# Macaron block on one core: the start-up DMAs move to SyncE, the weight setup becomes a planned step, and the whole order is replanned

## The reference

```
x = x + 0.5 * ffn(layernorm(x), gate_w, gate_b, w1, b1, w2, b2)      # stage A
x = x + attn(layernorm(x), Wq, Wkv_down, Wk_up, Wv_up, Wo)           # stage B
x = x + 0.5 * ffn(layernorm(x), gate_w, gate_b, w1, b1, w2, b2)      # stage C, the same weights

ffn:  probs = softmax(x @ gate_w.T + gate_b);  the 2 best of 8 experts
      y = sum over the 2 of prob * (relu(x @ w1[e] + b1[e]) @ w2[e] + b2[e])   # hidden size 256
attn: q = x @ Wq.T;  k, v = (x @ Wkv_down.T) @ W_up.T;  8 heads of 32, softmax over 512 tokens
```

## Time and profile before

| | |
|---|---|
| median of 3 runs | 1355.59 us (1354.84 to 1357.04) |
| the profiled execution | 1360.36 us, span 1358.6 us |
| mean granted TensorE clock | 0.948 of full |
| busy: PE | 1216.4 us (90%) |
| busy: DVE, POOL, ACT | 822.4, 795.4, 712.1 us |
| DMA | 203.12 MB, mean 150 GB/s |

### The profile page before, as it was taken

The page is one execution under the profiler, slowest core; times in us unless marked ns, Lnnn a source line. Parts: engine busy times, 40 slices in busy tenths (PEclk is TensorE's granted clock), DMA queues, the critical chain, the costliest instruction groups (busy, mean ns, idle before and its releaser), DMA issues.

```text
span 1358.6 us, 26424 instructions
## 1 busy us (share of the span) xinstructions
PE 1216.4 (90%) x8853; PEld 804.5 (59%) x8853; DVE 822.4 (61%) x2234; ACT 712.1 (52%) x1469; POOL 795.4 (59%) x783
## 2 busy tenths in 40 slices
PE   2888889999979989989989899999999988989893
PEld 1575466666655555556756565656565655657573
DVE  2745747686577655676638766764677836455242
ACT  1334556656645555656565456666555555545430
POOL 1012674765556757765385667768757675657633
PEclk9877999898989899989999899999998999989997
DMA  9204564762645165425645353544464327657741
GB/s 310 109 8 125 175 192 125 238 188 67 182 147 163 34 194 178 119 82 151 202 144 156 90 171 96 181 132 143 138 180 132 111 64 226 204 172 226 222 152 50
DMA packets 167913, 203.12 MB, mean 150 GB/s; under 512 B 17050, under 2 KB 112482, under 8 KB 167780
## 3 DMA queue, kind: packets, MB, share of 16 engines
q1 hardware_dynamic: 146944, 166.36, 39.9%
q0 software_dynamic: 15360, 31.49, 7.9%
q10 hardware_dynamic: 5476, 3.59, 0.8%
HBM read 153.53 MB, written 47.84 MB: 148 GB/s over the span
## 4 chain that ended last, share of the span: by engine, by line
PE 48%; POOL 15%; DVE 12%; issue 9%; DMA 9%; ACT 4%; ACTq 1%; SPq 1%; POOLq 0%; DVEq 0%
PE psum L1455 42%; POOL pairs L955 7%; POOL Y L1006 5%; DMA Y<-results_C,posC 4%; POOL slots_C L986 3%; DVE neg_m L1410 3%; DVE X L1394 3%; PE psum L1676 3%; DMA slots_C<-xnC,posC 2%; DMA Y<-results_A,posA 2%; ACT probs L1093 2%; PE psum L1554 1%; PE psum L1619 1%; PE psum L1518 1%; DVE ntC L1262 1%
## 5 line engine op out<-in xcount | busy, mean ns | idle before, releaser
L1410 DVE TENSOR_REDUCE neg_m<-psum 128x1 f32<-128x512 f32 x512 | 317.0, 682 | 175.2 <-PE psum L1455 137.6
L955 POOL TENSOR_TENSOR pairs<-probs 128x512 f32<-128x512 f32 x256 | 321.0, 1277 | 64.6 <-ACT probs L1093 61.1
L1455 PE MATMUL psum<-nat 32*128 32x512 f32 x2048 | 349.3, 641 | 7.0 <-DVE neg_m L1410 3.0
L1093 ACT ACTIVATE probs<-psum 128x512 f32<-128x512 f32 x512 | 264.6, 607 | 94.5 <-PE psum L1455 78.1
L986 POOL DMA_INDIRECT slots_A<-xnA,posA x120 | 117.2, 976 | 194.2 <-DVE posA L1378 84.7
L1455 PEld LDWEIGHTS psum<-nat 32*128 32x128 f32 x2048 | 137.4, 186 | 113.8 <-issue 38.3
L1455 PEld LDWEIGHTS psum<-xg_T,wt 128*128 128x128 f32 x1296 | 161.0, 198 | 40.3 <-issue 20.0
L1006 POOL DMA_INDIRECT Y<-results_C,posC x120 | 116.3, 969 | 114.0 <-DMA Y<-results_C,posC 74.3
L1455 PE MATMUL psum<-xg_T,wt 128*128 128x128 f32 x1296 | 177.9, 287 | 2.6 <-DMA wt<-packed 1.1
L986 POOL DMA_INDIRECT slots_C<-xnC,posC x120 | 118.5, 987 | 92.0 <-DMA slots_C<-xnC,posC 55.5
L1006 POOL DMA_INDIRECT Y<-results_A,posA x120 | 116.0, 967 | 87.2 <-DMA Y<-results_A,posA 51.0
(11 more groups left out here) (191 smaller groups left out, 1602.5 us busy)
## 6 DMA issues: line engine op xcount, KB each, us to landing
wt<-packed SPq DMA_DIRECT2D x324, 320.0 KB
xs<-slots_A SPq DMA_DIRECT2D x36, 256.0 KB
results_A<-ys SPq DMA_DIRECT2D x36, 256.0 KB
xs<-slots_C SPq DMA_DIRECT2D x36, 256.0 KB
results_C<-ys SPq DMA_DIRECT2D x36, 256.0 KB
X<-in_L_attn_x_dram SPq DMA_DIRECT2D x16, 256.0 KB, 5.3
out_dram<-X SPq DMA_DIRECT2D x16, 256.0 KB
packed<-probs SPq DMA_DIRECT2D x1, 2560.0 KB, 7.8
```

The costliest lines, as they stand in the source:

```text
L955: pool.tensor_tensor(pairs[:, kt // 2, j, :], probs[:, kt - 1, j, :], probs[:, kt, j, :], ALU.add).then_inc(S["p_added"], 1)
L1093: act.activation(probs[:, kt, j, :], at.banks()[j][:], ACT.Exp, scale=SCALE).then_inc(a_done, 1)
L1410: V_.tensor_reduce(neg_m[:, g, n, j:j + 1], at.banks()[j][:], AX.X, ALU.max, negate=True).then_inc(d_done, 1)
L1455: return nc.tensor.matmul(dst, w, m, start=start, stop=stop)
```

## The change

- The five attention weights, w1, b1, b2 and w2 are issued by SP in a new step `weights`, planned right behind the load of batch 0. ACT keeps the two gate DMAs, each now with a semaphore of its own.
- b1 comes as one row of 8 KB into one partition (`b1_row`). PE subtracts it from the sums: behind each product of `ones` with w1 follows one of `minus_one` (one row of -1) with `b1_row`, into the same bank. DVE needs one operation for each two experts instead of two.
- The setup is a planned step `setup` with parts on PE, ACT and DVE, behind `weights` and the first `logits`. ACT takes over the copies and high parts (`up_T`, `wqkv_h`, `wo_T`, b2's high parts); DVE keeps the subtractions.
- The gate is centred in two places: transposed before the first `xTf`, summed before the first `logits` (`center_gate`); DVE's `split_gate` runs behind the first `scaled`. POOL makes the identity and `ones` first and signals `ident_made`.
- The zeros are 992 elements wide and each is written 4 times per partition, instead of 256 wide, of which 128 are written 31 times. The second zeroing is planned behind the pack.
- All constants of the wanted times are new; `dh` no longer waits for the first `top1`.

```diff
-PERIOD, FIRST_B = 37.1, 69.39
+PERIOD, FIRST_B = 38.24, 39.26
-GROUP_GAP, MAX_PACE, S_FIRST, S_PACE, PV, ADD, SUM = 16.85, -0.47, 6.42, 3.29, -1.04, 48.06, 7.28
-A_LEAD, A_PACE, A_ROUTE, A_NORMS = 25.07, 8.22, 70.15, 8.3
-C_NORM, C_ROUTE, C_FIRST, C_PACE, C_GATHER = 54.52, 11.03, 52.26, 12.66, 13.88
-LOAD_AHEAD, W_AHEAD = 131.75, -1.62
-B_SHIFT = [-16.68, 10.52, -34.69, 26.01, 19.68, 22.99, -114.09, 39.85, 0.43, 9.81, 13.71, -5.78, -8.53, -28.27, 13.04, 118.28]
-A_SHIFT = [-30.75, -15.91, -16.67, -4.56, -2.89, -0.98, -3.68]
-C_SHIFT = [-12.0, 2.29, 20.79, -2.05, -93.81, 6.84, -64.33]
+GROUP_GAP, MAX_PACE, S_FIRST, S_PACE, PV, ADD, SUM = 15.72, -2.01, 5.9, 3.29, -0.74, 52.24, 4.01
+A_LEAD, A_PACE, A_ROUTE, A_NORMS = 36.46, 7.1, 71.69, 0.82
+C_NORM, C_ROUTE, C_FIRST, C_PACE, C_GATHER = 60.24, 5.64, 53.49, 12.44, 6.3
+LOAD_AHEAD, W_AHEAD = 121.7, -9.5
+B_SHIFT = [-12.96, 25.85, -23.82, 26.67, 22.19, -5.23, -81.66, 37.19, -12.29, -17.82, -36.02, -16.36, -4.18, -18.95, 34.18, 92.52]
+A_SHIFT = [-64.76, -32.85, 8.56, 1.55, 1.67, 0.78, -1.64]
+C_SHIFT = [-6.42, 7.83, 22.01, -28.41, -39.96, -80.33, -60.43]
...
+    "weights": ((("SP", 6.5),), 6.0), "setup": ((("PE", 4.0), ("ACT", 2.5), ("DVE", 6.0)), 0.0),
...
+    wanted["A", 0, "load", 0], wanted["A", 0, "weights", 0], wanted["A", 0, "setup", 0] = -1000.0, -999.0, -998.0
...
-    after(("A", 0, "pack", 0), ("A", 0, "top1", 0))
+    after(("A", 0, "weights", 0), ("A", 0, "load", 0), part=0)
+    after(("A", 0, "setup", 0), ("A", 0, "weights", 0), ("A", 0, "logits", 0))
+    for key in (("A", 0, "pack", 0), ("A", 0, "dh", 0), ("B", 0, "q", 0), ("A", 0, "top1", 0)):
+        after(key, ("A", 0, "setup", 0))
+    first_part(("A", 0, "blank", 0), ("A", 0, "weights", 0))
+    first_part(("A", 0, "blank", 1), ("A", 0, "pack", 0))
...
+            def weights(at):
+
+                for dst, src in (
+                    (wq_raw, wq.rearrange("(g p) d -> p g d", p=P)), (wo_raw, wo),
+                    (wk_raw, wk_up.rearrange("(g p) r -> p g r", p=P)),
+                    (wv_raw, wv_up.rearrange("(g p) r -> p g r", p=P)),
+                    (down_raw, wkv_down),
+                ):
+                    sp.dma_start(dst, src).then_inc(weights_in, 16)
+                sp.dma_start(pack[:, :, 0:HID], w1.rearrange("e p h -> p e h")).then_inc(experts_in, 16)
+                sp.dma_start(b1_row[:, 0:EXPERTS * HID], b1.rearrange("e h -> (e h)").unsqueeze(0)).then_inc(experts_in, 16)
+                for row in (0, B2_LOW):
+                    sp.dma_start(b2_raw[row:row + 1, 0:EXPERTS * D], b2.rearrange("e d -> (e d)").unsqueeze(0)).then_inc(experts_in, 16)
...
-                sp.dma_start(slots[s].rearrange("(p i) d -> p i d", p=P),
-                             zeros[:, 0:D].unsqueeze(1).to_broadcast([P, NT_MAX, D])).then_inc(zero_in[s], 16)
+                sp.dma_start(slots[s].rearrange("(p i) d -> p (i d)", p=P).rearrange("p (f c) -> p f c", f=4),
+                             zeros.unsqueeze(1).to_broadcast([P, 4, NT_MAX * D // 4])).then_inc(zero_in[s], 16)
...
+            def setup(at):
+
+                high_row, low_row = slice(0, 1), slice(B2_LOW, B2_LOW + 1)
+                act.wait_ge(setup_pe, 3)
+                act.activation(up_T, psum[5][0:RANK, :], ACT.Copy).then_inc(setup_act, 1)
...
-                    chain(V_.tensor_tensor(fix, fix, psum[i][:].rearrange("p (e h) -> p e h", e=2), ALU.subtract))
-                    V_.scalar_tensor_tensor(out=own, in0=fix, scalar=1.0 / D, in1=own, op0=ALU.mult, op1=ALU.add).then_inc(setup_dve, 1)
+                    V_.scalar_tensor_tensor(out=own, in0=psum[i][:].rearrange("p (e h) -> p e h", e=2), scalar=-1.0 / D, in1=own,
+                                            op0=ALU.mult, op1=ALU.add).then_inc(setup_dve, 1)
...
-                    pe_mm(psum[i][:].rearrange("p (e h) -> p e h", e=2), ones[:], pack[:, 2 * i:2 * i + 2, 0:HID]).then_inc(setup_pe, 1)
+                    pe_mm(psum[i][:].rearrange("p (e h) -> p e h", e=2), ones[:], pack[:, 2 * i:2 * i + 2, 0:HID], stop=False)
+                    pe_mm(psum[i][:], minus_one[:], b1_row[:, 2 * i * HID:2 * (i + 1) * HID], start=False).then_inc(setup_pe, 1)
...
+            def setup(at):
+
+                before = order["PE"][:order["PE"].index(at.step)]
+                pe.wait_ge(a_done, max(counts["a_full", step] for step in before if step[2] in A_STEPS))
+                pe.wait_ge(d_done, max(counts["d_full", step] for step in before if step[2] in D_STEPS))
+                turn_attention()
+                sum_experts()
```

More of the change, by code:

```diff
@@ L511, in assert_reuse @@
 def assert_reuse(order):
+    at_setup = {engine: order[engine].index(("A", 0, "setup", 0)) for engine in ("PE", "ACT", "DVE")}
+    for ring, engine in RELEASES.items():
+        names = D_STEPS if ring == "d" else A_STEPS
+        assert all(step in order[engine][:at_setup[engine]] for step in order["PE"][:at_setup["PE"]] if step[2] in names)
     at = {engine: {step: n for n, step in enumerate(order[engine])} for engine in ENGINES}
@@ L656, in macaron_kernel @@
     routed = [st[:2] for st in order["DVE"] if st[2] == "top1"]
-    first_steps = order["PE"][:order["PE"].index(("A", 0, "logits", 0)) + 1]
+    scaled_steps = [st for st in order["DVE"] if st[2] == "scaled"]
+    first_steps = order["PE"][:order["PE"].index(("A", 0, "setup", 0))]
     assert all(bank != GATE_BANK for step in first_steps for bank, _ in order["banks"][step])
@@ L1177, in _ @@
             chain = Chain(dve, link)
[L1179 to L1184 removed]
+            V_.memset(pack[:, :, B2C:WCOLS], 0.0).then_inc(b2_blank, 1)
             chain(V_.memset(b2_rows[:].bitcast(F32), 0.0))
@@ L1271, in scaled, with first_scaled @@
                 V_.tensor_scalar(plus[:], plus[:], -1.0, 0.0 if at.stage == "B" else 1.0, ALU.mult, ALU.add).then_inc(S["shift_done"], 1)
+            def first_scaled(at):
+                scaled(at)
+                if at.step == scaled_steps[0]:
+                    split_gate()
             def ring(at):
@@ L1430, in sum_ @@
                 V_.scalar_tensor_tensor(out=o, in0=o, scalar=-1.0, in1=r, op0=ALU.mult, op1=ALU.mult).then_inc(S["o_done"], 1)
-            def after_setup(does, parts):
-                def first(at):
-                    for part in parts.pop(at.name, ()):
-                        part()
-                    does[at.name](at)
-                return {name: first for name in does}
-            walk("DVE", after_setup({"norm": norm, "scaled": scaled, "xT": xT, "logits": logits, "top1": top1, "top2": top2,
+            walk("DVE", {"setup": setup, "norm": norm, "scaled": first_scaled, "xT": xT, "logits": logits, "top1": top1, "top2": top2,
                                      "rank1": rank1, "gate": gates, "rank2": rank2, "comb": comb, "wo": wo_,
-                                     "max": max_, "msplit": msplit, "sum": sum_, "dy": dy},
-                                    {"scaled": [split_gate], "top1": [split_attention, split_experts]}))
+                                     "max": max_, "msplit": msplit, "sum": sum_, "dy": dy})
         @block.tensor
@@ L1457, in turn_gate, with center_gate @@
             def turn_gate():
-                pe.wait_ge(gate_in, 32)
-                pe.wait_ge(consts_made, 1)
+                pe.wait_ge(gate_in, 16)
+                pe.wait_ge(ident_made, 1)
                 nc.tensor.transpose(psum[GATE_BANK][:, 0:EXPERTS], gw_raw, ident[0:EXPERTS, 0:EXPERTS]).then_inc(setup_pe, 1)
+            def center_gate():
                 pe.wait_ge(setup_dve, 1)
                 pe_mm(psum[GATE_BANK][:, EXPERTS:2 * EXPERTS], ones[:], gw_T[:]).then_inc(setup_pe, 1)
-            def emptied(last):
-                before = order["PE"][:order["PE"].index(last) + 1]
-                pe.wait_ge(a_done, max(counts["a_full", step] for step in before if step[2] in A_STEPS))
-                pe.wait_ge(d_done, max(counts["d_full", step] for step in before if step[2] in D_STEPS))
             def turn_attention():
@@ L1528, in logits @@
                 last.then_inc(d_full, 1)
-                if at.step == ("A", 0, "logits", 0):
-                    emptied(at.step)
-                    turn_attention()
-                    sum_experts()
             def rank1(at):
```

113 lines of the change are left out of this document (54 added, 59 removed).

## The result

The changed kernel is slower: its median is 1366.15 us (1360.73 to 1372.72) beside 1354.49 us of the kernel before in the same comparison, a ratio of **1.0108** (95% interval 1.0077 to 1.0138). A second comparison gave 1.0080 (1.0039 to 1.0120). The forecast was 1340.3 us with a range of 1330 to 1353: wrong in sign.

What follows compares the result with a forecast made beforehand. TensorE had room at the start (32 us, a chain behind ScalarE's DMA issues), middle (83, small waits) and end (21, gather backlog). Median 1355.6 less 15.3 (start 13.3, tail 2) gave 1340.3 us, range 1330 to 1353.

Steps and rivals of the forecast that it cites:

- (1): Start: ScalarE keeps two DMA issues and the table load, ready at 3.1 us; first logits' products end at 12.5 us.
- (2): Start: x of batch 1, queued behind eleven weight DMAs, lands at 13 us; TensorE's setup starts at 15.0 us.
- rival A: Start: the stall moves to SP, x1 lands at 19 instead of 13 us; total 1346.3 us; chance 0.14.
- (3): Setup: transposes 2.0 us, to 17.0; up_T's copy moves to ScalarE behind batch 1's scaled, done at 18.3 us.
- (4): Setup: low-rank product until 20.4 us, then eight sums (four with one-row b1) in 8.5 us, until 28.9 us.
- (5): Setup: VectorE's remaining subtractions behind the sums end at 31.2 us; first dense product at 31.3, 13.3 us earlier.
- The clock after the gap: First dense chunk: eight records took 6.59 us after idling, 3.68 behind busy TensorE; the 2.9 us difference counted as nothing.
- What the start wins moves all that follows: Whole kernel: nothing between 0 and 85 us but DMA is tied to absolute time, so the start's gain carries through.
- The replan: Middle and tail: new order leaves the middle unchanged within 8 us; tail gains 2 us, bounds -13 to +20.
- B: Tail: the backlog of gathers goes as well, worth 13 us; total 1329.3 us; chance 0.12.
- C: Tail: eight more expert quads left over behind B15, net 20 us slower; total 1360.3 us; chance 0.10.
- D: Middle: waits eat the gain, 97 us instead of 83; total 1354 us, no change; chance 0.08.

Runs made afterwards that it cites:

- e4: Changed kernel with b1's products over 128 rows, 127 of them zero, instead of one row; ratio 1.0039 to the kernel before.
- e5: Changed kernel with the old constants of the wanted times and b1's products over 128 rows; ratio 0.9939 to the kernel before.
- s2: Second run of e5 (changed kernel, old constants, b1's products over 128 rows); ratio 0.9893 to the kernel before.
- s4: Second run of e4 (changed kernel, b1's products over 128 rows); ratio 1.0022 to the kernel before.
- e9: Changed kernel with the old constants and eight more one-row products ahead of the sums; median 1361.02 us, ratio 1.0080 to the kernel before.
- e1: Changed kernel with all constants of the wanted times as they were before; ratio 0.9953 to the kernel before.
- p1: e1 with attention's sixteen shifts (B_SHIFT) each moved at random by at most 6; ratio 1.0241 to the kernel before.
- p2: e1 with attention's sixteen shifts each moved at random by at most 6, another draw than p1; ratio 1.0284 to the kernel before.
- e6: e1 with the new constants of stage C alone; ratio 1.0050 to the kernel before.
- e3: Changed kernel with the four products of ones first and the four one-row b1 products behind them; ratio 1.0103 to the kernel before.
- e7: e1 with the new constants of stage A alone; ratio 1.0271 to the kernel before.
- e8: e1 with the new constants of stage B alone, PERIOD and FIRST_B included; ratio 1.0410 to the kernel before.

## Why the prediction was wrong, step by step

**(1), ScalarE free at 3.1, logits' products done at 12.5: right.** Ln at 5.40, the products end at 12.33.

**(2), x1 at 13, setup at 15.0: right.** Statistics of batch 1 start at 13.69, the setup at 15.38. SP's queue did not hold x1 back, which was rival A.

**(3), `up_T` done at 18.3: right to half a microsecond.** It ended at 18.81.

**(4), eight sums in 8.5 us: the first step that failed.** They took 16.1 us (20.87 to 36.97). Both terms were mis-sized, by one cause, the one-row form between full products. I took the four full products as in the earlier trace rows, 5.07 us, though that figure already contained a rise of the clock: in that trace the records of the first two products start 0.85 to 1.0 us apart, and those of the last two 0.43 us. And I bounded a one-row product at 1.7 us, without asking what it does to the products between which it stands. e4 shows the cause: with 128 rows the eight take 9.6 us and the first dense product stands at 32.75 (33.68, 31.65 and 32.22 in e5, s2 and s4), near the 31.3 forecast. The one-row form cost 6 to 8 us: the low clock the larger part, the weight loads that it exposes the rest, 2.3 us by the estimate above.

**(5), VectorE behind the sums, 2.4 us: right,** 2.25. The gain of 13.3 us became 5.4. "Later than 38 us" was named as what would make the prediction wrong; it was 39.22.

The clock after the gap, counted as nothing, was nothing: the first eight dense records took 6.71 us for 6.59. (With full rows they took 5.34 us in e4, 5.32 in e5 and 3.67 in s2 and s4, where the clock was up before the gap.)

**What the start wins moves all that follows: right,** as far as the scatter lets it be seen: e9 shows 14.3 us (7 to 19) for 13.95 added.

**The replan, middle unchanged within 8 us, tail −2: the step that turned the sign.** From the first dense product to B15's end the changed kernel took 1277.0 us for 1247.9, +29.1; its tail 54.5 for 66.1, −11.6. Over the four profiles with new constants and the five with old ones (those of one changed structure), the middle is 1271 for 1235 us and the tail 54 for 66; the ratios, which rest on more executions, put the net at 1.3%, 18 us. The bound of 8 us was a tenth of the waits, and had no row behind it; e1 beside the changed kernel shows the true size of the term, and p1 and p2 (2.8% and 3.2%) show that some 40 us are possible by order alone. Every other order that was tried came out longer; why the one at hand is so good no run shows.

**The rivals.** B, the backlog of the tail gone (0.12), came true for the tail alone: TensorE's last product ends 3.7 us before the end instead of 21.4, and the tail is 11.6 us shorter, against 13 written. C, experts behind B15, hardly: from B15's `wo` to TensorE's last product 50.8 us for 44.7. D, waits in the middle (0.08), came true nearly to the figure: +14 us written, +13.3 measured. What D left out is that the same work then took 14.7 us more, because TensorE did more of it at the lower level of its clock. That term stood nowhere in the sum, and with it B, D and the short gain at the start make the result: −5.4 + 29.1 − 11.6 = +12.1 us of span, 1358.6 to 1370.7. The error was to treat B and D as alternatives: in e6 stage C's constants alone bring both, the short tail and the longer middle. That C's work in the middle is what lengthens it is argued and not shown; in p1 the middle is longer still with a tail of 64.5 us.

**What stays open.** Whether waits lower the clock or a lower clock makes the waits was not separated: no kernel here changed one and held the other. Nor is it known which steps of the new order collide; the loss is spread over many waits. A's and B's sets together without C's were not run.

## What to carry to other kernels

Do not price "everything is replanned" by a share of the idle time, and do not trust a planner's own end to rank two orders: here it saw 1.5 of 18 us. A random move of the priorities shows how far the order alone can carry the time (some 3% for moves of at most 6). Take a new structure and a new order apart, and keep the old order if the structure allows it; that alone turned 1.009 into 0.996, and with full rows into 0.989 to 0.994. Before a rank-one product is used to save VectorE a subtraction, look at what stands around it: here it held its neighbours at the low clock and exposed their weight loads, and spelling it with 128 rows, most of them zero, won 6 to 8 us.

## What the runs showed of the hardware

- One-row fp32 products of 512 columns did not raise TensorE's clock, alone (14 us in e9) or in turn with full ones (16 us in the changed kernel), and after full ones it fell (granted clock 1.00, 0.83, 0.50 in e3 while TensorE was busy throughout). With 128 rows in their place it rose (e4, e5, s2, s4).
- At the low level two products in a row start 1.71 us apart, of one row (e9) or of 128 with changing weights (e4), and 2.00 us where one-row and 128-row products take turns: there the weight load starts with its product and not beneath the one before.
- Before its first record of the clock a trace reads 1.00, whatever the level (products of 2.0 us at 1.00 in the first 40 us).
- Executions of one kernel differ with the mean granted clock: in 28 of the kernel before, from 0.952 to 0.962, the time fell by 9.9 us for each 0.01, and by 7 to 12 us in the other kernels with eight executions or more. Kernels with a worse order have a lower clock too (median 0.958 in e1, 0.950 in e7, 0.937 in e8).
- The issue of the weights on SP did not delay x1: batch 1's statistics started at 13.69 us with eleven DMAs in front of it, 3.1 MB in all.
